# Residual, layer norm, gate and expert ranking moved into the loop of the second edge walk, and expert lists built from 49 tiles of 128 nodes

## The reference, cut to what matters

```python
x = x + GAT(layernorm(x))             # two graph attention layers: 2 heads of 128, relu, then 1 head of 256
x = x + MoE(layernorm(x))             # per node: the 2 best of 8 experts, 256 -> 512 -> 256, exact gelu
x = x + GNN(layernorm(x))             # weighted mean over the edges, 2-layer MLP, layer norm
x = x + FFN(layernorm(x))             # 2 experts for the whole batch

# one attention layer
z = x @ W;  el, er = z . a_l, z . a_r
e = leaky_relu(el[src] + er[dst]);  ex = exp(e - segment_max(e)[dst])
out = segment_sum(z[src] * ex / segment_sum(ex)[dst]) + b

# the part that the change moves, after the second attention layer
x1 = x + agg / weight_sum + b2                     # residual
h  = (x1 - mean) / sqrt(var + 1e-5)                # layer norm
scores = h @ Wg + bg                               # gate, 8 columns
mask = the 2 highest of the 8 scores, as 0 and 1   # ranking
```

## Time and profile before

| | us |
|---|---|
| median of 3 runs (lowest to highest) | 4620.73 (4618.47 to 4625.1) |
| profiled execution | 4620.28 |
| its span in the trace | 4618.3 |
| busy: PE, PEld | 2847.1 (62%), 1811.1 (39%) |
| busy: POOL | 2690.4 (58%) |
| busy: DVE | 1989.9 (43%) |
| busy: ACT | 1530.8 (33%) |

### The profile page before, as it was taken

One profiled execution on the slowest core, in us unless ns is written; L12 is line 12 of the kernel. 1 busy time (PEld: TensorE's weight loads), 2 busy tenths in 40 slices (PEclk: granted clock), 3 DMA queues, 4 the chain that ended last, 5 costly groups with the idle time before them and its releaser, 6 DMA issues. The chain is left out here.

```text
span 4618.3 us, 59519 instructions
## 1 busy us (share of the span) xinstructions
PE 2847.1 (62%) x11768; PEld 1811.1 (39%) x11768; DVE 1989.9 (43%) x5676; ACT 1530.8 (33%) x4863; POOL 2690.4 (58%) x2734
## 2 busy tenths in 40 slices
PE   2346666666625555555554599932666666673999
PEld 2223333333312322223234488831433443442666
DVE  4266776776713434434447522244223223323222
ACT  1223333333312223222223033312455545552233
POOL 1177777777637777777732154523777777770221
PEclk9667777777857777777765899976888888885999
DMA  5556776777624444444435266677555555552111
GB/s 163 143 117 124 120 122 121 124 121 123 107 85 111 112 112 112 111 112 112 111 107 156 71 219 217 221 211 205 146 147 146 145 148 148 146 143 68 54 54 54
DMA packets 351633, 597.12 MB, mean 129 GB/s; under 512 B 83276, under 2 KB 241130, under 8 KB 350218
## 3 DMA queue, kind: packets, MB, share of 16 engines
q0 software_dynamic: 136224, 387.08, 36.7%
q1 hardware_dynamic: 179082, 169.94, 12.5%
q10 hardware_dynamic: 36160, 38.56, 2.7%
HBM read 486.83 MB, written 108.51 MB: 129 GB/s over the span
## 5 line engine op out<-in xcount | busy, mean ns | idle before, releaser
L588 POOL DMA_INDIRECT walk_rows<-z_two_heads,walk_idx x784 | 798.8, 1019 | 294.0 <-issue 229.6
L588 POOL DMA_INDIRECT walk_rows<-z_one_head,walk_idx x784 | 764.7, 975 | 328.0 <-issue 238.6
L1884 POOL DMA_INDIRECT walk_rows<-h,walk_idx x784 | 744.8, 950 | 268.9 <-issue 237.3
L2029 PE MATMUL walk_ps_part<-walk_rows,walk_whot 128*80 128x257 f32 x1568 | 505.5, 461 | 324.7 <-DMA walk_rows<-h,walk_idx 236.7
L698 PE MATMUL walk_ps_row_scores<-keep_ident,walk_rows 128*32 128x128 f32 (+1 forms) x98 | 35.5, 362 | 843.7 <-DMA walk_rows<-z_one_head,walk_idx 485.3
L735 PE MATMUL walk_ps_part<-walk_rows,walk_hot 128*80 128x258 f32 x1568 | 511.4, 457 | 0.0
L735 PE MATMUL walk_ps_part<-walk_rows,walk_whot 128*80 128x257 f32 x1568 | 472.7, 443 | 0.0
L2029 PEld LDWEIGHTS walk_ps_part<-walk_rows,walk_whot 128*80 128x80 f32 x1568 | 261.5, 182 | 501.6 <-issue 464.3
L698 PEld LDWEIGHTS walk_ps_row_scores<-keep_ident,walk_rows 128*32 128x32 f32 (+1 forms) x98 | 9.8, 100 | 881.9 <-issue 881.4
L601 ACT ACTIVATE walk_idx<-keep_src 128x8 int32 x212 | 44.2, 208 | 909.6 <-PE walk_ps_part L735 860.4
L735 PEld LDWEIGHTS walk_ps_part<-walk_rows,walk_whot 128*80 128x80 f32 x1568 | 251.6, 174 | 144.1 <-issue 92.0
(11 more groups left out here) (375 smaller groups left out, 4991.4 us busy)
## 6 DMA issues: line engine op xcount, KB each, us to landing
exp_w<-in_ffn_W SPq DMA_DIRECT2D x108, 512.0 KB
agg<-walk_window ACTq DMA_DIRECT2D x198, 80.3 KB
walk_rows<-z_two_heads,walk_idx POOLq DMA_INDIRECT x784, 4.0
walk_rows<-z_one_head,walk_idx POOLq DMA_INDIRECT x784, 2.8
comb_ya<-y_tokens POOLq DMA_DIRECT2D x28, 448.0 KB, 8.0
walk_rows<-h,walk_idx POOLq DMA_INDIRECT x784, 2.9
agg<-walk_window ACTq DMA_DIRECT2D x99, 80.6 KB
exp_b<-in_ffn_b SPq DMA_DIRECT2D x54, 128.0 KB
```

The lines of the kernel that those rows point to most:

```text
L588: pool.indirect_dma_start(out=Z[k // 2][:, k % 2 * GROUP_TILES + t, :], out_offset=None, in_=table, in_offset=bass.IndirectOffsetOnAxis(ap ...
L1884: pool.indirect_dma_start(out=Z[k // 2][:, k % 2 * GROUP_TILES + t, :], out_offset=None, in_=table, in_offset=bass.IndirectOffsetOnAxis(ap ...
L2029: last = pe.matmul(P[k % 2][0:WIN, 0:HW], S[k % HOTS][:, t, :], Z[k // 2][:, k % 2 * GROUP_TILES + t, :], start=t == 0, stop=t == GROUP_TI ...
```

## The change

The stage post is gone. A class PostRows does its work as the node work of walk2, one tile of 128 nodes a pair, with the hooks described above:

- SP: for tile v, two loads (rows of `agg`, rows of x) behind the store of its window and behind `x1_ready2`; two stores (x1, h) of tile v - 1.
- VectorE, behind `scores`: `normed(v-1)`, `rank_experts(v-1)`, `residual(v)`. The tile's number for the mask is a value_load from a new table `seqtile`, made in plan.
- ACT, behind the pair's 16 scales: a square root of 128 x 1 (`root`) and a copy of 256 columns (`features`).
- PE: two transposes of h (`turn`) and two matmuls of 8 columns (`products`).
- The tiles that remain run behind the last window (`rest_act`, `rest_pe`, `rest_dve`; the code that stood there becomes methods of SecondRows for walk1).
- The mask is 128 x 52 x 8 now, 49 of the 52 in use. dispatch works with 128 partitions, on 7 lists of 7 tiles, so with 14 `is_col` and 14 products for each list. x1, h and the input x are padded to 6656 rows.

The core of the diff:

```diff
+class PostRows:
...
+    def load(self, sp, v, k, row, stored, count):
+        if stored is not None:
+            sp.wait_ge(stored, count)
+            sp.sem_inc(self.tick, 1)
+        sp.wait_ge(self.x1_ready2, v + 1)
+        sp.sem_inc(self.tick, 1)
+        sp.dma_start(self.a[k][:, :], self.agg[bass.ds(row, TILE), 0:D + 1]).then_inc(self.rows_in[k], 16)
+        sp.dma_start(self.x[k][:, :], self.x_in[bass.ds(row, TILE), :]).then_inc(self.rows_in[k], 16)
+
+    def store(self, sp, v, k, row):
+        sp.wait_ge(self.h_ready1, v + 2)
+        sp.sem_inc(self.tick, 1)
+        sp.dma_start(self.x1d[bass.ds(row, TILE), :], self.x1[k][:, :]).then_inc(self.landed[k], 16)
+        sp.dma_start(self.hd[bass.ds(row, TILE), :], self.h[k][:, :]).then_inc(self.landed[k], 16)
...
+    def root(self, act, v):
+        act.wait_ge(self.var_ready, v + 1)
+        act.activation(self.mv[:, 1:2], self.mv[:, 1:2], ACT.Sqrt).then_inc(self.std_ready, 1)
+
+    def features(self, act, p):
+        act.wait_ge(self.turned1, p + 2)
+        act.wait_ge(self.gate_done1, p + 1)
+        act.activation(self.hT[:, :, :], self.psT[:, 0:HALVES * TILE].rearrange("p (h n) -> p h n", h=HALVES),
+                       ACT.Copy).then_inc(self.hT_ready1, 1)
+
+    def head(self, act, p, k):
+        self.root(act, p)
+        self.features(act, p)
...
+    def turn(self, pe, p, k):
+        pe.wait_ge(self.h_ready1, p + 1)
+        pe.wait_ge(self.hT_ready1, p + 1)
+        for hf in range(HALVES):
+            last = pe.transpose(self.psT[:, hf * TILE:(hf + 1) * TILE], self.h[1 - k][:, hf * 128:(hf + 1) * 128], self.ident[:, :])
+        last.then_inc(self.turned1, 1)
+
+    def products(self, pe, p, k):
+        pe.wait_ge(self.hT_ready1, p + 2)
+        pe.wait_ge(self.ranked1, p + 1)
+        for hf in range(HALVES):
+            last = pe.matmul(self.psG[:, 0:EXPERTS], self.hT[:, hf, :], self.Wg[:, hf, :], start=hf == 0, stop=hf == HALVES - 1)
+        last.then_inc(self.gate_done1, 1)
...
+    def residual(self, dve, v, k, turn):
+        dve.wait_ge(self.rows_in[k], turn * 32 + 32)
+        dve.tensor_scalar(self.inv[:, :], self.a[k][:, D:D + 1], 1e-30, None, ALU.max)
+        dve.tensor_tensor(self.x[k][:, :], self.x[k][:, :], self.brow[:, :], ALU.add)
+        dve.drain()
+        dve.reciprocal(self.inv[:, :], self.inv[:, :])
+        dve.drain()
+        dve.wait_ge(self.landed[k], turn * 32 + 32)
+        dve.scalar_tensor_tensor(self.x1[k][:, :], self.a[k][:, 0:D], self.inv[:, 0:1], self.x[k][:, :], ALU.mult, ALU.add)
+        dve.drain().then_inc(self.x1_ready2, 1)
+        dve.bn_stats(self.stats[:, :], self.x1[k][:, :])
+        dve.drain()
+        dve.bn_aggr(self.mv[:, :], self.stats[:, :])
+        dve.drain()
+        dve.tensor_scalar(self.mv[:, 1:2], self.mv[:, 1:2], LN_EPS, None, ALU.add)
+        dve.drain().then_inc(self.var_ready, 1)
+
+    def normed(self, dve, v, k):
+        dve.wait_ge(self.std_ready, v + 1)
+        dve.reciprocal(self.rstd[:, :], self.mv[:, 1:2])
+        dve.drain()
+        dve.wait_ge(self.turned1, v + 1)
+        dve.tensor_scalar(self.h[k][:, :], self.x1[k][:, :], self.mv[:, 0:1], self.rstd[:, 0:1], ALU.subtract, ALU.mult)
+        dve.drain().then_inc(self.h_ready1, 1)
+
+    def rank_experts(self, dve, p):
+        tile = dve.value_load(self.tile[0:1, bass.ds(p, 1)], min_val=0, max_val=UNITS_END - 1)
+        dve.wait_ge(self.gate_done1, p + 2)
+        dve.tensor_tensor(self.sc[:, :], self.psG[:, 0:EXPERTS], self.bg[:, :], ALU.add)
+        dve.drain().then_inc(self.ranked1, 1)
+        three = [TILE, EXPERTS, EXPERTS]
...
+        dve.tensor_tensor(self.mask[:, bass.ds(tile, 1), :].rearrange("p o e -> p (o e)"), self.rank[:, :], self.limit[:, :],
+                          ALU.is_lt)
+        dve.drain()
...
+    def scale(self, dve, v, k, turn):
+        self.normed(dve, v - 1, 1 - k)
+        self.rank_experts(dve, v - 1)
+        self.residual(dve, v, k, turn)
...
-def after_attention(nc, io, keep, dram):
...
-    TT = CHUNKS * CT
+    TT, LIST = NODE_TILES, 7
+    LISTS = TT // LIST
...
-        PER = 2 * CT
+        PER = 2 * LIST
...
-            "walk2": lambda: edge_walk(nc, keep, dram, "walk2", dram["z1"], 1),
-            "post": lambda: after_attention(nc, io, keep, dram),
+            "walk2": lambda: edge_walk(nc, keep, dram, "walk2", dram["z1"], 1, lambda ph: PostRows(ph, io, keep, dram)),
```

More of the change, by code:

```diff
@@ L451, in scale, with first, rest_act, rest_pe @@
         dve.drain().then_inc(self.h_ready2, 1)
+    def first(self, dve):
+        self.scale(dve, 0, 0, 0)
+    def rest_act(self, act, u, left, half):
+        self.head(act, u, 1)
+        self.copy_out(act, u, 1, half)
+        with act.Fori(0, left) as i:
+            for k in range(2):
+                self.head(act, i * 2 + (u + 1 + k), k)
+                self.copy_out(act, i * 2 + (u + 1 + k), k, i + (half + 1))
+    def rest_pe(self, pe, u, left):
+        self.turn(pe, u, 1)
+        self.products(pe, u, 1)
+        with pe.Fori(0, left) as i:
+            for k in range(2):
+                self.turn(pe, i * 2 + (u + 1 + k), k)
+                self.products(pe, i * 2 + (u + 1 + k), k)
@@ L675, in _ @@
             if node:
[L676 to L683, removed]
+                node.rest_act(act, n * PAIRS + 1, pairs_left(act), n * (PAIRS // 2))
             act.wait_ge(stored, n * (16 * UNROLL) + 48)
@@ L776, in _ @@
             if node:
[L777 to L784, removed]
+                node.rest_pe(pe, n * PAIRS + 1, pairs_left(pe))
         @block.vector
@@ L913, in _ @@
             if node:
-                node.scale(dve, 0, 0, 0)
+                node.first(dve)
             for m in range(PAIRS):
@@ L924, in _ @@
             if node:
[L925 to L930, removed]
+                node.rest_dve(dve, n * PAIRS + 1, pairs_left(dve), n * (PAIRS // 2))
 def pipeline(eng, *stages):
@@ L1369, in _ @@
                     last = pe.matmul(psL[:, 0:SLOT_COLS], is_row[c % 2][:, u, :], is_col[c % 2][:, u, :],
-                                     start=c == 0 and u == 0, stop=c == CHUNKS - 1 and u == PER - 1)
+                                     start=c == 0 and u == 0, stop=c == LISTS - 1 and u == PER - 1)
                 last.then_inc(listed2, 1)
@@ L1456, in _ @@
                 last.then_inc(made, 1)
-            dve.wait_ge(listed2, CHUNKS)
+            dve.wait_ge(listed2, LISTS)
             dve.tensor_copy(who[:, :], psL[:, 0:SLOT_COLS])
@@ L2475, in _ @@
             chunks(dve, finish)
-PHASES = ("plan", "rows1", "walk1", "walk2", "post", "dispatch", "experts", "combine", "walk3", "route", "ffn")
+PHASES = ("plan", "rows1", "walk1", "walk2", "dispatch", "experts", "combine", "walk3", "route", "ffn")
 def program(nc, io, out):
```

308 lines of the change are left out of this document (135 added, 173 removed).

## The result

The changed kernel takes **4481.55 us** (median of four runs, 4477.82 to 4485.64) beside 4619.6 of the kernel before on the same chip: a ratio of 0.9695, with a 95% interval of 0.9683 to 0.9706. The forecast was 4567, its range 4505 to 4640.

A forecast was written before the change was run, and what follows sets the result against it. POOL's indirect gathers were taken to bound the second walk now. From 4620.28 us, -164.4 (post) - 5.5 (dispatch) + 71 (walk) + 8 (its end) + 38 (tail) = -53 gave 4567 us, range 4505 to 4640.

The forecast's parts named there:

- the sum of the walk: Second walk, first to last gather: 13 pairs at 20.8 us and nine turns of 89.2, 1073 against 1002, so +71.
- The tail: Three tiles left after the second walk's last store take 41 us, as in the first walk: +38, bounds 28 and 45.
- Post and dispatch: Removing the post stage saves 164.4 us; dispatch, with 7 lists of 14 columns, saves 5.5, between 0 and 7.
- The new work on VectorE: Per pair of the second walk, normed 0.9, rank_experts 2.3 and residual 2.7 us: 6.0 together, bounds 5.2 and 7.0.
- The table loads: ACT alternates Exp and Sqrt in the second walk: two function table loads a pair, 1.30 us each, both in the chain.
- The ring: Second walk, logits to next pair's logits through ACT, PE and VectorE: 20.2 us a pair, bounds 19.2 and 21.8.
- The stop at the back edge: VectorE stops at the second walk's loop end, once in four pairs: 8.4 us for each of nine back edges.
- Gathers: POOL's gathers in the second walk get longer beside new VectorE operations: 0.3 us a pair, 0 to 1.2, making 20.8.
- The end of the walk: PE's last two pairs of the second walk wait for ACT's copies: +8 us, bounds 0 to 13.
- no stop, or one that slack absorbs: Rival: no loop stop counts in the second walk, POOL bounds it, +17 and +4 at the end: 4510 us; chance 0.21.
- The long ring: Rival: the second walk's per-pair chain eats the gain from 21.4 us; at 21.9 the time is 4643; chance 0.19.
- the tiles behind the walk: Rival: all 49 tiles run after the second walk, at about 9 us each: over 4800 us; chance 2 in 100.

The follow-up runs named there:

- exp_load_late: Changed kernel with one Sqrt of 128 x 1 on ScalarE between the wait for the logits and the second walk's Exp; 4548.87 us.
- after: The changed kernel itself, with the post stage's work moved into the second walk, against the kernel before; 4481.55 us, ratio 0.9695.
- dve_plus_4: Changed kernel with four more copies of 128 x 256 with drains on VectorE behind the residual; 4552.61 us.
- dve_plus_2: Changed kernel with two more copies of 128 x 256 with drains on VectorE behind the residual; 4514.16 us.
- code_shift_60: Changed kernel with 60 writes of one element on VectorE ahead of the first walk's loop, moving its later code; 4463.96 us.
- before_long_loop: Kernel before with 22 writes of one element on VectorE per pair of the second walk, making its loop 311 instructions; 4628.99 us, ratio 1.0001.

## Why the prediction was right and wrong

What failed is the sum of the walk: +71 was forecast and -2.3 measured, because a turn of four pairs took 82.0 us and not 89.2. The tail, +24.7 for +38, is the second miss.

- **Post and dispatch**: right, -164.5 and -5.9 (forecast -164.4 and -5.5). A list takes 5.40 us (L1494 at 2450.08 less 2444.68, its start for the list before; forecast 5.45).
- **The new work on VectorE**: right, 5.7 (forecast 6.0). The value_load was undersized (0.5, with 0.8 as upper bound, for an idle 0.82 that also holds a drain), `residual` oversized (2.3 for 2.7).
- **The table loads**: half wrong. "2 x 1.30 us a pair, both in the chain" failed for Exp. The earlier trace rows showed a load behind a wait, and the prediction made that a rule; here the load runs ahead of the wait. exp_load_late shows that its place counts.
- **The ring**: 20.2 was forecast, and the loop of `after` averages 19.4. Link by link the fast pair has 6.4 (ACT; forecast 7.8), 1.8 (PE; 2.3), 3.2, 5.9 and 0.9, in all 18.2. Where the ring was made to bound the walk, it is 19.8 (dve_plus_4) to 20.2 (dve_plus_2) less what was added. The mechanism was right; that the size came so near is partly luck: ACT's link was 1.4 too long, mostly Exp's load, and PE's, 3.1 in those kernels, 0.8 too short. In the check on VectorE alone the terms leave 11.0, not 10.7, so 19.1 and not 18.8; the ring is still the longer.
- **The stop at the back edge**: it came, and in the place that was forecast, but at half the size, 4.25 for 8.4. It was copied from the first walk on the ground of the loop's length; code_shift_60 and before_long_loop show that length alone doesn't make it, so that it came at all is partly luck.
- **The two together** are the miss. A turn was forecast at 4 x 20.2 + 8.4 = 89.2 and took 82.0, which is POOL's pace: 4.2 us from the stop and 3.0 from the ring. Nine turns make 65 of it; the 13 pairs outside them took 262 (1000.1 less 9 x 82.0) for 270, 8 more: together the 73 between the forecast walk of 1073 and 1000.1. The experiments put the sizes back in part, and the gathers pay as the forecast said, and a little more: 34.6 us for 3.0 more in the stop (nine times 3.0 is 27), 31.2 for 0.7 more in the ring (36 times 0.7 is 26).
- **Gathers**: 0.3 us of stretch a pair was forecast, none came. Summed over the trace, gathers longer than 1.02 us exceed 0.95 by 17.9 us in all (18.1 before), and 17.8 of it stands in L1019, the old L817. None of the new operations is among them but one L610, with 0.1.
- **The end of the walk**: 12.8 for 8, within its bounds of 0 to 13. **The tail**: 24.7 for 38, below its lower bound of 28. The term was taken over from the first walk's tail; a tile takes 6.4 us here (2378.47 to 2384.86, the starts of two residuals), and only three stand in the chain.
- **The rivals**: the first ("no stop, or one that slack absorbs") is what happened to the walk, by its second half, with next to no slack over. Its 4510 was too high by the gathers (+17 against -2.3) and the tail, and too low by 9 at the end of the walk. With one of the two terms at its forecast size a turn would be 85 to 86, half the loss; with both smaller there is none. The prediction gave this case 0.21. The long ring and the tiles behind the walk did not come.
- **Its own test**: "I am wrong if POOL still never waits" was the sign to look for, and it came true.

## What to carry to other kernels

Where a stage is paced by one engine, find the pace of the next-slowest ring as well, add up all that happens once per loop turn, and state the distance between the two: in this kernel the change was free up to that knee and more work cost more than its size behind it, and a few tenths of a us per pair decided which. Measure such a stage to its end: buffers with a lead hide the lag from the engine that paces it until the lead is gone. A cost that is copied from another loop (a stop, a tail) needs its own bounds, since its size belongs to that loop's place and order. A function table load counted here only where ScalarE had no wait to hide it in.

## What was not expected of the hardware

The stop of 7 to 10 us at a loop's back edge, nine times in the first walk, vanished when the same 311 instructions lay 60 further on, and with it 6 to 28 us of the stage, though POOL had hardly waited for VectorE there. The Trainium skill (Runtime: NRT & Kernel Launch, Instruction fetch mechanics) has a branch back wait where its target lies outside two blocks of 256 instructions; that the place decides agrees with it. The loop of 367 instructions stopped in each of the three places that were tried. By a count of the program's instructions, with one offset common to all of the loops, the rule doesn't give these stops and the first walk's together; what decides stays open.
